# A mixture-of-experts routing whose exponentials are transposed by VectorE and DRAM instead of TensorE

## What is computed

```
xn = layernorm(x1, gamma, beta)
logits = (xn / |xn| * scale) @ (mu / |mu|)          # [tokens, 256 slots]
dispatch = softmax(logits, axis=tokens); combine = softmax(logits, axis=slots)
slot_in  = dispatch^T @ xn                          # [256 slots, 256]
slot_out = gelu(slot_in @ w1 + b1) @ w2 + b2        # per expert
out      = layernorm(x1 + combine @ slot_out)
```

## Time and profile before

| | us |
|---|---|
| median of three runs (622.67 to 622.85) | 622.74 |
| the profiled execution's own time | 622.77 |
| its span, first to last instruction | 621.0 |
| granted TensorE clock, mean over the span, of full speed | 0.997 |
| attention, to about | 414 |
| routing, to about | 546.6 |
| experts, to about | 558.1 |
| mixing, to the end | 621.0 |

### The profile page before, as it was taken

The page is one execution under the profiler, slowest core; times in us unless marked ns, Lnnn a source line. Parts: engine busy times, 40 slices in busy tenths (PEclk is TensorE's granted clock), DMA queues, the critical chain, the costliest instruction groups (busy, mean ns, idle before and its releaser), DMA issues. The chain is left out here.

```text
span 621.0 us, 12379 instructions
## 1 busy us (share of the span) xinstructions
PE 605.4 (97%) x4100; PEld 558.0 (90%) x4100; DVE 426.0 (69%) x948; ACT 412.4 (66%) x920; POOL 342.5 (55%) x359
## 2 busy tenths in 40 slices
PE   7999999999999999999999999989999999999995
PEld 5989989989999999999998999989999999988884
DVE  5377677677676776777777768897555556347876
ACT  4756767667677667776776776676766666535674
POOL 1737658568485585574855856766434433103443
PEclk9999999999999999999999999999999999999998
DMA  8301012012020210110201201020000000302444
GB/s 228 104 2 69 6 63 70 1 69 69 0 68 1 66 68 0 68 65 3 68 0 68 68 2 35 1 56 15 1 1 0 0 0 1 69 1 69 148 158 169
DMA packets 29326, 30.21 MB, mean 49 GB/s; under 512 B 5326, under 2 KB 25196, under 8 KB 29292
## 3 DMA queue, kind: packets, MB, share of 16 engines
q1 hardware_dynamic: 29280, 29.78, 15.0%
q10 hardware_dynamic: 12, 0.00, 0.0%
HBM read 21.39 MB, written 8.39 MB: 48 GB/s over the span
## 5 line engine op out<-in xcount | busy, mean ns | idle before, releaser
L488 POOL TENSOR_TENSOR h_lo<-xn_all,h_hi 128x512 fp32r<-128x512 f32 x32 | 41.4, 1294 | 126.1 <-ACT xn_all L565 126.0
L563 ACT ACTIVATE h_hi<-bank,bias_col 128x512 fp32r<-128x512 f32 x96 | 66.3, 691 | 35.2 <-PE bank L690 31.8
L1067 DVE TENSOR_TENSOR state_lo<-bank,state_hi 128x512 fp32r<-128x512 f32 x57 | 39.2, 688 | 60.9 <-ACT state_hi L604 60.9
L688 PE MATMUL bank<-xnT_hi,w_hi 128*128 128x512 f32 x188 | 76.1, 405 | 0.0
L690 PE MATMUL bank<-xnT_hi,w_lo 128*128 128x512 f32 x188 | 74.3, 395 | 0.0
L689 PE MATMUL bank<-xnT_lo,w_hi 128*128 128x512 f32 x188 | 74.3, 395 | 0.0
L1460 PE MATMUL bank<-xn_all,e_tok 128*128 128x257 f32 x256 | 66.4, 382 | 0.5 <-ACT slot_inT L1388 0.3
L1365 ACT ACTIVATE e_tok<-bank,shift,xinv 128x256 f32<-128x256 f32 x64 | 36.1, 564 | 45.0 <-PE bank L1443 24.8
L1540 DVE COPY ET_all<-bank 128x256 f32<-128x256 f32 (+1 forms) x64 | 27.0, 424 | 53.3 <-PE bank L1454 52.9
L604 ACT CAST state_hi<-bank 128x512 fp32r<-128x512 f32 x57 | 33.5, 587 | 39.2 <-PE bank L830 39.1
L1532 PE MATMUL bank<-w_sb,ET_all 128*128 128x256 f32 x256 | 55.4, 380 | 0.0
(11 more groups left out here) (192 smaller groups left out, 2080.7 us busy)
## 6 DMA issues: line engine op xcount, KB each, us to landing
x_all<-in_L_attn_x SPq DMA_DIRECT2D x16, 512.0 KB, 3.5
xn_all<-in_xT SPq DMA_DIRECT2D x15, 512.0 KB, 4.4
out<-xn_all SPq DMA_DIRECT2D x15, 512.0 KB, 3.0
w_sb<-in_L_ffn_w SPq DMA_DIRECT2D x2, 512.0 KB, 5.2
xn_all<-in_L_ffn_w SPq DMA_DIRECT2D x2, 512.0 KB, 6.2
xn_all<-in_xT SPq DMA_DIRECT2D x2, 256.0 KB, 3.6
out<-xn_all SPq DMA_DIRECT2D x2, 256.0 KB, 2.5
x_all<-in_L_attn_W2k SPq DMA_DIRECT2D x1, 258.0 KB, 4.4
```

Of the source, the lines that this page charges most:

```text
L488: pool.tensor_tensor(h_lo[:, V_SLOT, m, :], hv[:, m, :], h_hi[:, V_SLOT, m, :].bitcast(F32), ALU.subtract).then_inc(hv_split, 1)
L563: nc.scalar.activation(h_hi[:, h_slot(j, n), m, :], ps, ACT.Gelu, bias=bias(n, m))
L688: nc.tensor.matmul(ps, w[0], xs[0], start=start, stop=False, skip_group_check=shared)
L1067: nc.vector.tensor_tensor(lo[:, :, :], state_halves, hi[:, :, :].bitcast(F32), ALU.subtract).then_inc(state_split, 1)
```

## The change

TensorE no longer transposes the exponentials and VectorE no longer copies them. VectorE transposes `e_tok` in blocks of 32x32 (`turn_e`) into one of two buffers `e_turn`, in which the four tiles of a group lie interleaved: element order is slot block, token within 32, tile. When a group's four tiles are turned, SP stores the buffer (512 KB, pieces of 512 B) to a scratch in DRAM, waits until it has landed, and loads it back with four DMAs of 32 partitions each into `ET_all`, so that slots lie on the partitions. All 16 exchanges stand in SP's queue, w2's two loads between the 14th and the 15th. TensorE waits for all 64 loads before the mixing, and takes its weights from `ET_all` with a step of four words. The exponential (ScalarE) waits for the turn of four tiles earlier, the turn waits for the store of two groups earlier. VectorE's order in a group changes as the diff shows. In the first group, the sum of mu's squares stands ahead of the projection of v, its power ahead of GpSimd's addition of ln_b, and its factors between the two bias additions of v.

```diff
@@ attention: GpSimd, TensorE, VectorE
                         if more:
                             split_x(g + 1)
+                        if not attend:
+                            invert_mu_norms()
                         add_ln_b(g)
...
+                    if not attend:
+                        sum_mu_squares()
                     project_v(g, j, 0)
...
                     if not attend:
                         pe.wait_ge(moe_loaded, 16 * 6)
                         turn_moe_biases()
-                        sum_mu_squares()
...
+                    else:
+                        floor_mu()
                     bias_v(g, j, 0)
+                    if not attend:
+                        mu_factors()
@@ routing: buffers
-            ET_all = msb("ET_all", [P, SB, TILES * P])
+            ET_all = msb("ET_all", [P, GROUPS * SB * GT, GT * 32])
+            QUAD, PATCHES = 32, ES // 32
+            e_turn = [msb(f"e_turn{i}", [P, PATCHES, QUAD, GT]) for i in range(2)]
+            e_scratch = nc.dram_tensor("e_scratch", [GROUPS, PATCHES, P, GT * QUAD], F32, kind="Internal").ap()
@@ routing: SP
-                sp.wait_ge(tile_folded, TILES + TB // 2)
-                for w in range(2):
-                    sp.dma_start(w2_sb[w * H:(w + 1) * H, :, :],
+                def exchange_e(g):
+                    sp.wait_ge(e_turned, GT * g + 2 * GT)
+                    sp.dma_start(e_scratch[g].rearrange("f p n -> p f n"),
+                                 e_turn[g % 2][:, :, :, :].rearrange("p f c t -> p f (c t)")).then_inc(e_stored, 16)
+                    sp.wait_ge(e_stored, 16 * g + 16)
+                    for f in range(PATCHES // SB):
+                        sp.dma_start(
+                            ET_all[QUAD * f:QUAD * f + QUAD, g * SB * GT:(g + 1) * SB * GT, :],
+                            e_scratch[g].rearrange("(f s) (j r) n -> f r (s j) n", s=SB, r=QUAD)[f]
+                        ).then_inc(eT_loaded, 16)
+
+                for g in range(GROUPS):
+                    exchange_e(g)
+                    if g == GROUPS - GB // 2 - 1:
+                        sp.wait_ge(tile_folded, TILES + TB // 2)
+                        for w in range(2):
+                            sp.dma_start(w2_sb[w * H:(w + 1) * H, :, :],
@@ routing: ScalarE
                     act.wait_ge(logits_done, TB * b + t + 1)
+                    act.wait_ge(e_turned, TB * b + t + 1)
@@ routing: TensorE
                     pe.wait_ge(e_ready, TB * b + t + 3)
-                    pe.wait_ge(eT_ready, TB * b + t + 1)
-                    if t < 2:
-                        pe.wait_ge(z_ready, TILES + GT - 2 + 2 * t)
-                    for s in range(SB):
-                        last = nc.tensor.transpose(eT_ps[t % 2][:, s * P:(s + 1) * P],
-                                                   e_tok[:, t % 4, s * P:(s + 1) * P], ident[:, :])
-                    last.then_inc(eT_done, 1)
@@ mixing: TensorE
-                pe.wait_ge(eT_ready, TILES + 2)
+                pe.wait_ge(eT_loaded, 16 * GT * GROUPS)
...
-                            last = nc.tensor.matmul(mix_ps[k % 2][t][:, 0:D], ET_all[:, s, toks],
+                            at = (SB * k + s) * P // QUAD
+                            group = ET_all[:, at:at + P // QUAD, :].rearrange("p j (c t) -> p t (j c)", t=GT)
+                            last = nc.tensor.matmul(mix_ps[k % 2][t][:, 0:D], group[:, t, :],
@@ routing: VectorE
+                def turn_e(b, t):
+
+                    g = GB * b + t // GT
+                    if t % GT == 0 and not (isinstance(b, int) and b == 0 and t < 2 * GT):
+                        dve.wait_ge(e_stored, 16 * g - 16)
+                    dve.wait_ge(e_ready, TB * b + t + 3)
+                    nc.vector.transpose(
+                        e_turn[t // GT % 2][:, :, :, t % GT].rearrange("p (f s) c -> p f s c", s=SB),
+                        e_tok[:, t % 4, :].rearrange("p (s f c) -> p f s c", s=SB, c=QUAD)).then_inc(e_turned, 1)
...
-                        if t == TB - 1:
-                            normalise_slots(b)
-                        if t % GT == 1 and not (last and q == GB - 1):
+                        if t % GT == 1 and not (last and q == GB - 1) and not (first and q == 0):
+                            split_xnT(dve, k + 1, (q + 1) % GB)
+                        if t % GT == 2 and not (last and q == GB - 1) and not (first and q == 0):
                             floor_norms(dve, k + 1, (q + 1) % GB)
...
-                        if t % GT == 3 and not (last and q >= GB - 2):
-                            split_xnT(dve, k + 2, (q + 2) % GB)
+                    normalise_slots(b)
```

More of the change, by code:

```diff
@@ L501, in split_v, with invert_mu_norms @@
                                        ALU.subtract).then_inc(v_split, 1)
+                def invert_mu_norms():
+                    pool.wait_ge(mu_floored, 1)
+                    pool.tensor_tensor(mu_inv[:, :], mu_n2[:, :], minus_half[:, 0:SB], ALU.pow).then_inc(mu_rs, 1)
                 def body(g, j, ba, attend=True, project=True, settle=True, more=True):
@@ L1231, in build @@
             e_ready = msem("e_ready")
-            eT_done = msem("eT_done")
-            eT_ready = msem("eT_ready")
+            e_turned = msem("e_turned")
+            e_stored = msem("e_stored")
+            eT_loaded = msem("eT_loaded")
             tile_folded = msem("tile_folded")
@@ L1239, in build @@
             slot_inT_ready = msem("slot_inT_ready")
[L1241 removed]
+            log_ps, fold_ps = bank[2:4], bank[4:6]
             LEAD = 2
@@ L1290, in _ @@
                                  ).then_inc(w1_loaded, 16)
-                sp.wait_ge(tile_folded, TILES + TB // 2)
-                for w in range(2):
-                    sp.dma_start(w2_sb[w * H:(w + 1) * H, :, :],
-                                 w2.rearrange("(r two) h d -> two h r d", two=2)[w]).then_inc(w2_loaded, 16)
+                def exchange_e(g):
[14 more added lines that the diff above has]
+                            sp.dma_start(w2_sb[w * H:(w + 1) * H, :, :],
+                                         w2.rearrange("(r two) h d -> two h r d", two=2)[w]).then_inc(w2_loaded, 16)
                 for k in range(LAST):
@@ L1307, in _ @@
             def _(pool):
-                for n, (starts, at) in enumerate(((e_ready, 2), (tile_folded, TB), (eT_ready, 2),
+                for n, (starts, at) in enumerate(((e_ready, 2), (tile_folded, TB), (e_turned, GT),
                                                   (slot_inT_ready, SB))):
@@ L1332, in _ @@
                 pool.wait_ge(tile_folded, TILES + TB)
+                pool.wait_ge(e_turned, TILES + GT)
                 for w in range(2):
@@ L1547, in route @@
                         q, k = t // GT, GB * b + t // GT
-                        copy_eT(b, t)
-                        if first and t == 3:
+                        turn_e(b, t)
+                        if first and t == 4:
                             z_summed(dve, a, 0)
                             z_statistics(a, p, 0)
-                        if first and t == 4:
+                        if first and t == 5:
                             z_summed(dve, a, 1)
                             z_statistics(a, p, 1)
-                        if first and t == 6:
+                        if first and t == 7:
                             z_deviation(dve, a, p)
-                        if first and t == 9:
+                        if first and t == 10:
                             shift_z(dve, a, p)
-                        if t == TB - 1:
-                            normalise_slots(b)
-                        if t % GT == 1 and not (last and q == GB - 1):
+                        if t % GT == 1 and not (last and q == GB - 1) and not (first and q == 0):
+                            split_xnT(dve, k + 1, (q + 1) % GB)
+                        if t % GT == 2 and not (last and q == GB - 1) and not (first and q == 0):
                             floor_norms(dve, k + 1, (q + 1) % GB)
@@ L1594, in _ @@
                 split_xnT(dve, 1, 1)
+                floor_norms(dve, 1, 1)
                 dve.wait_ge(x1_ready, TILES - GT + 2 * GT)
```

15 lines of the change are left out of this document (1 added, 14 removed).

## The result

The changed kernel takes 613.77 us (median of four runs, 613.64 to 614.52), the kernel before, run beside it, 622.80. The ratio is 0.9855, 95% interval 0.9838 to 0.9872: 9.0 us faster. Forecast were 609.1 us, 13.7 us faster. The direction and the range hold; a third of the gain is missing.

What follows compares the result with a forecast made beforehand. TensorE, 97% busy, was taken to bound the kernel in routing and mixing. Savings of 14.1 - 0.7 - 1.2 + 1.5 = 13.7 us from 622.77 gave 609.1 us, range 606.5 to 620.

Steps and rivals of the forecast that it cites:

- rivals 1 to 3: Routing loop sets pace, 616 us, chance 0.08; last exchange late before mixing, 613, 0.11; exchange loop bounds routing, about 620, 0.05.
- Transposes leave TensorE: Routing: removing 0.22 us of transposes per tile over 64 tiles saves 14.1 us, less 0.7 at three batch boundaries.
- VectorE turns blocks: Routing: VectorE's turn takes 0.6 us a tile (bounds 0.42 to 0.85), hidden under TensorE's 7.16 us per group.
- rival 1: Routing: exponentials, norms and GpSimd's power set the pace; half the transposes' gain turns into waits, 616 us; chance 0.08.
- The first group: Start of the routing: VectorE's split for tile 8's logits ends late, at 428.9, losing 1.2 us of the gain once.
- The exchange: DRAM round of 5.3 us per group hidden by routing, 0 us; last exchange before mixing hidden with 2.6 us to spare.
- Mixing reads its weights with a stride: Mixing: weight loads reading every fourth word cost 0 us; upper bound +28 us, called the largest unknown.
- rival 4: Mixing: strided weight loads slow it past break-even at 0.27 us a load; at three times 637.5 us; chance 0.16.
- Opening: First group's start: earlier mu norms remove TensorE's 1.26 us idle at L916 and 0.2 before attention; 1.5 us gained.

Runs made afterwards that it cites:

- e7_pieces128: The changed kernel with four stores of 128 B pieces per group, turns writing each tile's tokens side by side, mixing weights read straight: 620.83 us.
- e10_pairs: The changed kernel with mu's factors and diagonal on ScalarE, plus two tiles interleaved instead of four (256 B pieces, weights at every second word): 608.81 us.
- e9_parted: The changed kernel with mu's factors and diagonal on ScalarE, plus exchange loads into a one-group buffer that GpSimd copies apart into ET_all, weights read straight: 617.13 us.

## Why the prediction was partly right

The direction was right, and so was the mechanism of the main gain. The range held in part by luck: it was drawn for rivals 1 to 3, none of which came, and the two losses that did come, at the weights and in the opening, were put at nothing or not seen; that they summed to less than its width was not foreseen.

**Transposes leave TensorE: right.** Folds are 1.57 us apart (456.57, 458.14), and a group takes 7.18 us (454.12 to 461.30) where 7.16 stood. Of 14.1 us, 12.9 arrived, where I had 12.2. At the boundaries 0.8 are lost, for 0.7: the three pairs of transposes across the first gave 0.43 instead of 0.66 (8.02 us from one transposing of tokens to the next, now 7.59), the 36 across the other two 7.33 instead of 7.92.

**VectorE turns blocks: right.** 0.647 us for 0.6; VectorE is busy 25.91 of 33 us, 79%, where 5.5 of 7.16, 77%, were forecast. ScalarE's waits did not grow (45.0 us before the exponentials, now 32.7), and TensorE is busy for 32.43 of the 33 us, with 0.57 of idle at the batch boundary in them, so rival 1 is out. But the reason for my value was wrong. I argued from L158 that hopping costs nothing; the turn takes 0.445 us at step 1 (e7_pieces128), 0.446 at step 2 (e10_pairs) and 0.647 at step 4. The Trainium skill (Vector Engine (DVE) Microarchitecture Reference, section 5.2) has 2.5 ns an element for a destination that steps by 24 words, and no row for four; the estimate from it, 0.79 us, has the right sign and is too much in size.

**The first group: wrong cause.** I had VectorE's split for tile 8 end too late, 1.2 us lost. It ended at 428.17, 0.5 ahead of its logits at 428.67, since back to back three turns take 1.56 us, not 1.8. 0.4 us were lost all the same (0.22 gained over the first three tiles, for 0.66): from 416.68 on ScalarE works without a pause at exponentials, squares and roundings, and TensorE, faster now, waits for it at tile 4's logits (421.58), which start 1.23 us behind the fold before them (420.35), where 0.80 stood.

**The exchange: right.** SP's queue at the end of the routing, and the DMA issues of the page (KB each, median us to landing):

```profile
522.85 1.78 SPq L1306 DMA_DIRECT2D ET_all<-e_scratch  x4
524.68 1.40 SPq L1316 DMA_DIRECT2D xn_all<-in_L_ffn_w  x2
526.81 0.39 SPq L1302 DMA_DIRECT2D e_scratch<-e_turn  x1
534.37 1.79 SPq L1306 DMA_DIRECT2D ET_all<-e_scratch  x4
536.21 0.45 SPq L1302 DMA_DIRECT2D e_scratch<-e_turn  x1
539.87 1.78 SPq L1306 DMA_DIRECT2D ET_all<-e_scratch  x4
```

```profile
e_scratch<-e_turn SPq DMA_DIRECT2D x16, 512.0 KB, 3.2
ET_all<-e_scratch SPq DMA_DIRECT2D x64, 128.0 KB, 2.8
```

The store lands after 3.2 us (3.3), the four loads are issued in 1.8 (1.8). The last turn ends at 533.08; against it w2's issue ends at -7.0 (forecast -7.0), the loads behind store 14 begin at +1.3 (+0.3), the last are issued at +8.6 (+7.8), and by their 2.8 us have landed near +11, before +12.9. About 2 us to spare instead of 2.6. With pieces of 256 B (e10_pairs) they are gone.

**Mixing reads its weights with a stride: the step that failed.** "I take 0", by L158. The mechanism was named, in rival 4, with the right place. Its threshold (a load is free until 0.216 us) holds for the distance at which loads follow each other, not for their records: at step 3 a record of 0.251 us still cost nothing. And its price fell between forecast and rival: loads follow each other at 0.234, 18 ns over the matmul, times 240 is the 4.3 us. The nearest row was a read by VectorE at a step of 1 KB. It could not speak for TensorE's reads at 16 bytes, and as a bound from below it was no reason to take zero. The prediction's estimate from the same 2.5 ns of the Trainium skill, which that section measured on VectorE, was 0.32 us a load and 27 us in all. The record is 0.329 us, but records overlap, and the distance that sets the time is 0.234.

**Opening: the second step that failed.** "L916 follows L801 directly. Gain 1.26". It gained 0.1 us instead of 1.5. I priced VectorE's and GpSimd's operations by the durations that each has while the other stands still, though the change moved three of VectorE's from a stretch where GpSimd stood still (from 31.69, GpSimd's power having ended at 31.66) into one where it adds without a pause. I also had not counted v's second bias, which now stands behind them in VectorE's queue, with ScalarE and TensorE behind it. In place of the 1.26 us there is an idle of 1.43.

The sum: 13.7 forecast, less 4.3 for the weights, less 1.4 for the opening, plus 0.7 for the routing and 0.2 in the tail, which I did not follow, is 8.9; measured are 9.0.

## What to carry to other kernels

When a layout changes to suit one engine or the DMA, price it at every reader: a step that makes transfers cheap may be paid at each weight load, and the step next to it may be free. Look for the price in a row of the same engine and the same step; where there is none, keep the range open and test it alone, which took one line of code here. And before an operation is moved in time, look at what the other engine of the pair VectorE and GpSimd does in its new place: small operations on SBUF operands can take as long as the other's large ones.

## What was not expected of the hardware

- VectorE's operations on SBUF operands waited for GpSimd's to end: 2.32 us for two that take 0.48 (mu_diag), 1.32 for one of 0.23, while ScalarE did those two in 0.70, and VectorE's own with an input in PSUM kept 0.69.
- A weight load's record by step of its words, 128 columns of fp32: 190 ns at 1, 196 at 2, 251 at 3, 329 at 4, 337 at 8, 307 at 16. A turn of 128x256 by VectorE: 445 and 446 ns written at steps 1 and 2, 647 at 4.
- Four stores in pieces of 128 B in place of one in pieces of 512 B, four times as many pieces, made a round of the exchange 7.65 us instead of 5.0 (3.2 to land, 1.8 to issue the loads): by far less than four times, and all of it in the 3.2 us that SP took to issue the four.
- A wait of TensorE cost more than itself: after 4.8 us at a standstill (e9_parted) the granted clock fell to 0.50, the level of 1.2 GHz, for some 3.5 us, another 1.6 us of time; after 8.7 us (e7_pieces128) for some 6.5 us, another 1.9.
